# A constant-fed start of TensorE, and a new order of the weight splits, in the opening of a two-layer kernel

## What is computed

```python
def _L0_attn_ref(data, mask, weight, bias):      # s: a linear layer whose weight is masked in 32x32 blocks
    bm = mask.reshape(Nb, BH, Kb, BW).sum(axis=(1, 3)) > 0
    wb = weight.reshape(Nb, BH, Kb, BW) * bm[:, None, :, None].astype(weight.dtype)
    out = jnp.einsum('bsk,nk->bsn', data, wb.reshape(N, K)) + bias
def _L0_ffn_ref(x, c1_w, c2_w, w1, w2t):         # g: one of each 32 hidden units is picked per row
    inter = xf @ c1_w.T @ c2_w.T                 # rank 16, 1792 columns
    idx = jnp.argmax(blk, axis=-1) + jnp.arange(0, INTER, SPARSITY)
    h = jax.nn.relu(jnp.einsum('bkm,bm->bk', w1[idx], xf))
    out = jnp.einsum('bk,bkm->bm', h, w2t[idx])
```

## Time and profile before

| | before |
|---|---|
| median of 3 runs | 663.97 us |
| the profiled execution, its own time | 666.39 us |
| its span in the trace | 664.6 us |
| TensorE busy | 629.1 us (95%) |
| VectorE busy | 452.3 us (68%) |
| GpSimd busy | 238.1 us (36%) |
| ScalarE busy | 213.7 us (32%) |

### The profile page before, as it was taken

How to read it: one execution, slowest core, us unless ns; L and a number is a source line. 1 busy time by engine, 2 the same in 40 slices (tenths; PEclk the granted TensorE clock), 3 DMA queues, 4 the chain that set the end, 5 groups by cost and what they waited for, 6 DMA issues and landing times.

```text
span 664.6 us, 8396 instructions
## 1 busy us (share of the span) xinstructions
PE 629.1 (95%) x2910; PEld 511.2 (77%) x2910; DVE 452.3 (68%) x716; ACT 213.7 (32%) x379; POOL 238.1 (36%) x185
## 2 busy tenths in 40 slices
PE   2699999999999999999989898999999999999997
PEld 2478788778888878888768687678878878887887
DVE  6977775777775787765887685665756657485633
ACT  3423343412222312223313134553146125313610
POOL 1516555370000550000761245573514342351441
PEclk9899999999999999999999899999999999999999
DMA  8940000031500032300043522012130014002001
GB/s 236 404 180 1 0 1 0 1 96 32 149 19 8 8 96 60 113 16 8 25 134 97 172 80 72 17 67 108 42 127 23 1 47 142 0 32 96 2 28 37
DMA packets 42575, 46.16 MB, mean 69 GB/s; under 512 B 25072, under 2 KB 25456, under 8 KB 41904
## 3 DMA queue, kind: packets, MB, share of 16 engines
q1 hardware_dynamic: 42544, 45.76, 21.1%
HBM read 31.85 MB, written 8.39 MB: 61 GB/s over the span
## 4 chain that ended last, share of the span: by engine, by line
PE 80%; DVE 11%; issue 3%; DMA 3%; POOL 1%; ACT 1%; SPq 0%; DVEq 0%; POOLq 0%; ACTq 0%
PE bank L417 72%; PE bank L347 2%; DVE counts L928 2%; DVE seg_top L914 2%; DVE eq L916 1%; PE bank L1187 1%; DVE h_lo L958 1%; DMA first<-counts 1%; DVE h L949 1%; PE bank L1334 1%; PE bank L1169 1%; PE bank L1297 1%; DMA x_tile<-in_x 1%; DVE ws_lo L987 1%; DMA b_raw<-in_lora_b 1%
## 5 line engine op out<-in xcount | busy, mean ns | idle before, releaser
L417 PE MATMUL bank<-w_hi_t,h_hi 128*128 128x512 f32 x224 | 91.0, 406 | 4.0 <-DVE h_lo L958 3.8
L752 ACT ACTIVATE h_hi<-h 128x512 fp32r<-128x512 f32 x56 | 35.4, 632 | 166.1 <-DVE h L949 166.1
L417 PE MATMUL bank<-w_lo_t,h_hi 128*128 128x512 f32 x224 | 88.3, 394 | 0.0
L417 PE MATMUL bank<-w_hi_t,h_lo 128*128 128x512 f32 x224 | 87.9, 392 | 0.0
L417 PE MATMUL bank<-xT_hi,w_hi_t 128*128 128x512 f32 x224 | 87.5, 391 | 0.1
L417 PE MATMUL bank<-xT_lo,w_hi_t 128*128 128x512 f32 x224 | 87.2, 389 | 0.0
L417 PE MATMUL bank<-xT_hi,w_lo_t 128*128 128x512 f32 x224 | 87.2, 389 | 0.0
L928 DVE TENSOR_TENSOR_SCAN counts<-restart,eq 128x512 bf16<-128x512 bf16 (+1 forms) x56 | 74.6, 1333 | 2.4
L914 DVE TENSOR_REDUCE seg_top<-bank 128x16 f32<-128x512 f32 (+1 forms) x64 | 39.6, 618 | 52.7 <-PE bank L1187 52.7
L393 POOL TENSOR_TENSOR g_tile<-g_tile,s_tile 128x512 f32<-128x512 f32 x31 | 42.4, 1368 | 91.5 <-DVE g_tile L971 46.6
L958 DVE TENSOR_TENSOR h_lo<-h,h_hi 128x512 fp32r<-128x512 f32 x56 | 42.5, 758 | 29.4 <-ACT h_hi L752 27.8
(11 more groups left out here) (189 smaller groups left out, 1303.1 us busy)
## 6 DMA issues: line engine op xcount, KB each, us to landing
w_raw<-in_w SPq DMA_DIRECT2D x28, 256.0 KB, 9.4
x_res<-in_x SPq DMA_DIRECT2D x4, 1024.0 KB, 8.9
mid_state<-g_tile SPq DMA_DIRECT2D x16, 256.0 KB, 2.1
x_tile<-mid_state SPq DMA_DIRECT2D x4, 1024.0 KB, 7.5
x_res<-mid_state SPq DMA_DIRECT2D x4, 1024.0 KB, 5.6
out<-g_tile SPq DMA_DIRECT2D x15, 256.0 KB, 2.0
x_tile<-in_x SPq DMA_DIRECT2D x3, 1024.0 KB, 5.5
b_raw<-in_lora_b SPq DMA_DIRECT2D x2, 1024.0 KB, 5.1
```

What stands on the lines that cost most here:

```text
L417: last = nc.tensor.matmul(dst, a, b, start=(start and n == 0), stop=(stop and n == len(mms) - 1))
L752: nc.scalar.activation(h_hi[:, it % 2, :], h[:], ACT.Copy).then_inc(h_hi_done, 1)
```

## The change

Five edits, all in the opening:

- VectorE zeroes the segment heads of `restart` as its third instruction, and a semaphore of its own, `restart_in`, tells that `restart` is complete. The later waits on `consts_dve` count less accordingly.
- TensorE multiplies `restart` by itself, 28 times before it waits for the rows, and 4 times between the transposes of the rows and the rank product. The results go to bank 7 and are read by nobody.
- VectorE makes `ws_lo` right behind the masking of ws. Behind it come the segment maxima and the equality of the first selection, then the rest of c2's second part, then the first scan and the other selections.
- TensorE no longer waits for all four `ws_lo` ahead of the `s` products; in the first row block it waits for each block of k by itself.
- GpSimd waits for the rest of c2's second part before it goes on with w1[2], w2[0] and the others.

```diff
@@ constants and GpSimd
+        WARM = (28, 4)
             w1_rest(0)
             w1_rest(1)
+            gp.wait_ge(c2_split, 2)
             for it in range(2, IT + 2):
@@ VectorE
-            nc.vector.memset(restart[:], 2.0).then_inc(consts_dve, 1)
+            nc.vector.memset(restart[:], 2.0).then_inc(restart_in, 1)
             nc.vector.memset(restart_e[:], 2.0).then_inc(consts_dve, 1)
+            dve.wait_ge(restart_in, 1)
+            nc.vector.memset(restart[:].rearrange("p (s n) -> p s n", n=SEG)[:, :, 0:1], 0.0).then_inc(restart_in, 1)
             nc.vector.memset(c2_f, 0.0).then_inc(c2_zero, 1)
...
-            dve.wait_ge(consts_dve, 4)
-            nc.vector.memset(restart[:].rearrange("p (s n) -> p s n", n=SEG)[:, :, 0:1], 0.0).then_inc(consts_dve, 1)
+            dve.wait_ge(consts_dve, 3)
...
-            c2_rest(1)
             for k in range(KD):
                 dve.wait_ge(ws_hi_done, k + 1)
                 nc.vector.tensor_tensor(ws_lo[:, k, :], ws_raw[:, k, :], ws_hi[:, k, :].bitcast(F32),
                                         ALU.subtract).then_inc(ws_split, 1)
+            select_largest(0, 0, 0)
+            c2_rest(1)
+            select_count(0, 0, 0)
+            for tt in range(1, TT):
+                select(0, 0, tt)
             dve.wait_ge(c2_split, 2)
-            for tt in range(TT):
-                select(0, 0, tt)
             body(0, False)
@@ TensorE
-                three(s_bank(c, tt)[:], [(xT_hi[:, k, rows(tt)], xT_lo[:, k, rows(tt)], ws_hi[:, k, :], ws_lo[:, k, :])
-                                      for k in range(KD)]).then_inc(s0_done, 1)
+                for k in range(KD):
+                    if early and tt == 0:
+                        pe.wait_ge(ws_split, k + 1)
+                    last = three(s_bank(c, tt)[:], [(xT_hi[:, k, rows(tt)], xT_lo[:, k, rows(tt)], ws_hi[:, k, :], ws_lo[:, k, :])],
+                                 start=(k == 0), stop=(k == KD - 1))
+                last.then_inc(s0_done, 1)
...
+            def keep_going(n):
+
+                for _ in range(n):
+                    nc.tensor.matmul(banks[7][:], restart[:, 0:P], restart[:], start=True, stop=True)
+
+            pe.wait_ge(restart_in, 2)
+            keep_going(WARM[0])
             pe.wait_ge(consts_gp, 6)
             for tt in range(TT):
                 if tt == TT - 1:
                     pe.wait_ge(xT_done, 1)
                 transpose_rows(pe, 0, tt)
+            keep_going(WARM[1])
             pe.wait_ge(c1_split, 1)
...
             up_product(0, 1, True)
-            pe.wait_ge(ws_split, KD)
             for tt in range(TT):
                 s_product(0, tt, True)
```

More of the change, by code:

```diff
@@ L216, in block_mask_ffn_then_attention_lora_kernel @@
         consts_dve = sem("consts_dve")
+        restart_in = sem("restart_in")
         ld_x_first = sem("ld_x_first")
@@ L886, in _ @@
             dve.wait_ge(ld_mask, 16)
-            dve.wait_ge(consts_dve, 10)
+            dve.wait_ge(consts_dve, 8)
             with nc.allow_low_precision(reason="counts of ones"):
```

## The result

The changed kernel takes 657.48 us (median of six runs, 656.26 to 659.98) where the kernel before takes 664.16 us (six runs, 662.97 to 666.09): a ratio of 0.9892, with a 95% interval of 0.9867 to 0.9917. The forecast was 657.5 us. The profiled execution took 658.42 us, its span is 656.6 us, against 666.39 and 664.6.

A forecast was written before the change was run, and what follows sets the result against it. TensorE was taken to be held by a 5.96 us wait for `ws_lo` and the low clock behind it. Earlier rows and splits, limited by selections and scan collisions, gave 6.5 us: 663.97 - 6.5 = 657.5 us, range 655.5 to 660.8.

The forecast's parts named there:

- The bound: TensorE idles 5.96 us until the last `ws_lo`, held up by GpSimd's splits; the clock falls, slowing the first `s` product.
- Part 1: TensorE's opening: 28 constant products raise the clock and end at 10.8 us, before the rows at 11.3, delaying nothing.
- Part 2: Transposes of the rows: at the high clock, they move everything behind them up by about 1.0 us.
- Part 3: Splitting ws behind its mask: last `ws_lo` ready at 25.35 us, not 30.67; first `s` product ends at 26.4, not 36.12.
- Part 4: Selections on VectorE become the bound: transposes of the counts could start at 37.65 us, 7.45 us earlier.
- Part 5: GpSimd's splits beside the scans: first scan free, second and third lose 0.6 to 0.8 us each; first down product 6.5 us earlier.
- The sum: Whole kernel: the first down product's 6.5 us gain comes through to the end, giving a median of 657.5 us.
- Products too late: Rival, chance 0.09: opening clock rises late, constant products end at 14.35 us; gain only 2.4 us, time 661.6 us.
- Slow splits for another reason: Rival, chance 0.06: `ws_lo` stay at 1.74 us because of ScalarE or loads, not GpSimd; gain 3.4 us, time 660.6 us.
- The gain lost again: Rival, chance 0.05: the gain vanishes at a later point tied to the loads or DMA queue; time 664 us.
- The clock falling in the new waits: Rival, chance 0.05: TensorE's 1.2 us gaps between `s` products lower the clock; 4.1 us lost, time 668.1 us.

The follow-up runs named there:

- GpSimd's wait alone: The kernel before with one added line: GpSimd waits for the four `ws_lo` before splitting w1[2] and the rest; ratio 0.9951 to before.
- GpSimd in the gaps: The changed kernel with GpSimd's first four w splits released behind the last `ws_lo` and the first three scans, instead of all behind c2; 655.93 us.

## Why the prediction was right

**The bound.** Right. GpSimd's wait alone turned `ws_lo` from 5.7 to 2.5 us, and in the changed kernel the low clock went with the hole. With GpSimd's wait alone a gap of 3.00 us and a low clock stayed.

**Part 1.** Right in its outcome: the products ended at 9.99, not 10.8. Its margin is thinner than one profile tells: in the executions with 28 of them they took 7.50 to 9.12 us, so the gap ahead of the rows was 0.47 to 2.33 us, and in two of them (2.05 and 1.99 us) the clock fell again.

**Part 2.** 1.02 us forecast as 1.0. Taken out of the changed kernel it is 0.67; where the clock had fallen ahead of the rows (the gap of 1.99 us) the rank product came 0.9 later.

**Part 3.** Right; masking at 19.21 and `ws_lo` of 2.48 us instead of 2.85, 0.5 us together on their end (24.82 against 25.35). The wait by block of k, which it used, turned out to carry nothing. Its closest neighbour, the landing of w1[1], was named with 0.3 us of room. In two executions w1[1] came 0.15 us too late. The load ahead of it, w1[0], which the prediction gave no room, came 0.30 to 0.71 us too late in three.

**Part 4.** Right, and it is what made the forecast: the 9.7 us of the first `s` product shrink to 7.5 or less because the selections become the bound. The single wait for ws, 1.1 us later and free, shows it directly.

**Part 5.** Right by mechanism and nearly by size: the first scan free, the second and third at +0.83 and +0.84 us where 0.6 to 0.8 was put, 1.67 against 1.5. With GpSimd in the gaps they vanished to the hundredth. The page of the Trainium skill named with the forecast (GPSIMD Engine Reference, 8. Key points) says that instructions with two SBUF inputs contend; in every run here the pairs that read PSUM kept their 0.68 and 0.69 us beside GpSimd, and the two-SBUF ones lost up to 1.1 us when they came second, and nothing when they came first. `h_lo` went free too (0.68 us, 0.7 forecast).

**The sum.** In the trace the first down product moved 7.5 us, not 6.5: against the forecast 0.5 more on masking and `ws_lo`, 0.2 on the selections, 0.2 on TensorE's own work behind them, and 0.1 from the rounding of the terms. The medians moved 6.7 us, with an interval of 5.5 to 8.8, in which both lie. So the match of the median to 0.02 us is luck within that interval; that size and place agree within 1 us is not.

**The rivals.** Products too late: not in these kernels, but 44 of them show its price, 2.1 us where it had said 4.1 (the transposes were fast behind them, not slow). Slow splits for another reason: refuted. The gain lost again: not up to the second chunk, whose rank product also came 7.5 us earlier. The clock falling in the new waits: not in this kernel, whose gaps are 1.25 us at most, but it can from 2.0 us on, and the change's order without GpSimd's wait ran into it. What the rival was weighed against, that the clock had held for 4.3 us of idle time, was one execution's value: in the gap of 2.69 us it fell some 2.3 us after TensorE had stopped (0.92 on average over the 2.70 us).

## What to carry to other kernels

When a hole closes, find the next engine on the path before adding up the gain; a part that hurries work ahead of that engine (here the wait by block of k) is worth nothing. Where two engines hold each other up, as VectorE and GpSimd do here, it is cheapest to release the one's instructions where the other reads PSUM, which a semaphore that already exists can do; but each held-back instruction has to be placed, or it collides further on. What a part of a change is worth depends on what stands beside it, and one profiled execution can hide it (the products: 1.5 us later alone, 0.67 us earlier in the finished kernel), so take parts out one at a time from the finished kernel as well as adding them to the old one.

## What the runs showed of the hardware

The granted clock fell in gaps shorter than the 4.3 us that the kernel before suggested. The longer gaps behind a busy TensorE at the high level, in the first 60 us of the profiled executions, and what the clock did:

| gap of TensorE, us | clock |
|---|---|
| 1.13, 1.22, 1.25, 1.38, 1.60, 1.61, 1.72 | stayed high |
| 1.99, 2.05, 2.69 | fell |
| 2.33, 2.70, 2.79 | stayed high |
| 3.00, 5.96, 5.97, 6.94 | fell |

From 1.99 to 2.8 us it went either way, and in the runs with 1.99, 2.05 and 3.00 us the low level began only after TensorE was back at work (0.1, 0.5 and 1.2 us after). The rise varied too: the 28 products, the same in every kernel, took 7.50 to 9.12 us. And the landing of w1[0], issued near 5.5 us, moved between 14.0 and 17.2 us over the profiled executions of all kernels (14.0 and 14.4 in the two of the changed kernel), as much as most of the edits here are worth.
